# Normalisations on GpSimd, the values' bias through the output projection, and the gate in the output weights

## What is computed

```python
mod = (silu(c) @ wmod).reshape(4, 6, 1, 256)
sa, ca, ga, sb, cb, gb = mod[:, 0], ..., mod[:, 5]
ga = (2 * (ga >= 0) - 1) * maximum(abs(ga), 0.25)         # gb likewise
h = layernorm(x) * (1 + ca) + sa
qkv = h @ Wqkv.T + bqkv                                    # causal softmax attention per head
x = x + ga * (attention(qkv) @ Wout.T + bout)
h = layernorm(x) * (1 + cb) + sb
x = x + gb * ffn(h)                                        # shared + top-1 of 8 experts
```

## Time and profile before

| | |
|---|---|
| median of 3 runs | 481.53 us (480.63 to 483.06) |
| the profiled execution | 479.8 us |
| its span, first to last instruction | 478.1 us |
| first exponential of blocks 0, 1, 2, 3 | 69.55, 121.81, 183.48, 237.13 us |
| mean granted TensorE clock | 0.967 |
| busy: TensorE, VectorE, ScalarE, GpSimd | 402.4, 310.0, 226.8, 209.0 us |

### The profile page before, as it was taken

The page is one execution under the profiler, slowest core; times in us unless marked ns, Lnnn a source line. Parts: engine busy times, 40 slices in busy tenths (PEclk is TensorE's granted clock), DMA queues, the critical chain, the costliest instruction groups (busy, mean ns, idle before and its releaser), DMA issues.

```text
span 478.1 us, 8357 instructions
## 1 busy us (share of the span) xinstructions
PE 402.4 (84%) x2898; PEld 227.9 (48%) x2898; DVE 310.0 (65%) x629; ACT 226.8 (47%) x403; POOL 209.0 (44%) x251
## 2 busy tenths in 40 slices
PE   3767677889978789988879968999968999999991
PEld 3233233444544345444434434565645666666661
DVE  3823697876898968999977753789734444444441
ACT  2533424867666666755677636345122232323220
POOL 1457393374226763358331762110600555555332
PEclk9997789999999999998999989999989999999998
DMA  8568548765678557652433001994621344434210
GB/s 258 170 154 212 147 117 259 265 196 136 168 264 293 156 127 167 222 179 88 169 81 99 2 0 52 354 360 161 180 86 44 65 80 85 78 74 81 32 21 0
DMA packets 45921, 67.95 MB, mean 142 GB/s; under 512 B 5365, under 2 KB 33653, under 8 KB 45881
## 3 DMA queue, kind: packets, MB, share of 16 engines
q1 hardware_dynamic: 40200, 58.76, 40.6%
q0 software_dynamic: 5152, 8.14, 8.6%
q10 hardware_dynamic: 528, 0.52, 0.3%
HBM read 43.14 MB, written 25.18 MB: 143 GB/s over the span
## 4 chain that ended last, share of the span: by engine, by line
PE 51%; DVE 17%; DMA 8%; POOL 7%; issue 7%; ACT 6%; SPq 3%; ACTq 0%; DVEq 0%; POOLq 0%
PE bank L1411 35%; DVE mx L1066 5%; PE bank L1525 4%; PE bank L1509 3%; DVE rowg L1167 2%; PE bank L1739 2%; PE bank L1481 2%; DMA qk_d<-W 2%; POOL W L719 2%; DMA w_d<-rowg 2%; DMA mod_d<-h2T 1%; ACT rowg L896 1%; DMA stage<-in_gup 1%; POOL rowg L727 1%; POOL rowg L726 1%
## 5 line engine op out<-in xcount | busy, mean ns | idle before, releaser
L846 ACT ACTIVATE W<-bank 128x512 f32<-128x512 f32 (+1 forms) x176 | 94.8, 564 | 65.1 <-PE bank L1509 63.3
L1066 DVE TENSOR_REDUCE mx<-bank 128x1 f32<-128x384 f32 (+3 forms) x176 | 104.8, 632 | 20.2 <-PE bank L1483 19.9
L1411 PE MATMUL bank<-W 128*128 128x256 f16 (+2 forms) x756 | 106.5, 293 | 10.2 <-POOL W L694 3.4
L1411 PEld LDWEIGHTS bank<-W 128*128 128x128 f16 x756 | 73.3, 100 | 44.3 <-issue 14.2
L1481 PE MATMUL bank<-W 126*128 126x128 f16 (+3 forms) x256 | 67.0, 318 | 20.6 <-DVE mx L1066 17.2
L719 POOL TENSOR_SCALAR_AFFINE_SELECT W<-W 128x512 f32<-128x512 f32 x64 | 45.3, 713 | 79.7 <-ACT W L846 79.7
L1411 PE MATMUL bank<-W,h2T 128*128 x276 | 68.4, 385 | 4.9 <-DVE W L1182 4.0
L1509 PE MATMUL bank<-W 128*128 128x512 f16 (+3 forms) x256 | 63.1, 304 | 5.2 <-ACT W L846 3.5
L789 POOL DMA_INDIRECT out<-h2T,sidx x23 | 36.3, 1578 | 69.5 <-DVE h2T L1381 69.2
L1525 PE MATMUL bank<-W 128*32 128x128 f32 (+3 forms) x512 | 48.4, 451 | 8.7 <-POOL W L719 8.7
L1483 PE MATMUL bank<-maskb,identb 128*128 128x128 bf16 (+2 forms) x176 | 45.3, 257 | 0.0
(11 more groups left out here) (163 smaller groups left out, 522.7 us busy)
## 6 DMA issues: line engine op xcount, KB each, us to landing
w_d<-rowg SPq DMA_DIRECT2D x18, 512.0 KB, 3.9
W<-w_d SPq DMA_DIRECT2D x18, 512.0 KB, 8.0
stage<-in_gup SPq DMA_DIRECT2D x16, 512.0 KB
qk_d<-W SPq DMA_DIRECT2D x48, 128.0 KB
W<-qk_d SPq DMA_DIRECT2D x32, 192.0 KB, 4.4
stage<-in_down SPq DMA_DIRECT2D x8, 512.0 KB
x_sb<-in_x SPq DMA_DIRECT2D x4, 512.0 KB, 8.9
h_d<-gbb SPq DMA_DIRECT2D x4, 512.0 KB, 4.5
```

The costliest lines, as they stand in the source:

```text
L846: a.activation(PT[j][:, i:i + m, :], t_bank(N)[:, 0:m * w].rearrange("p (i n) -> p i n", i=m), ACT.Exp).then_inc(s_exp, 1)
L1066: v.tensor_reduce(mx_v[:, b % 2, hp0 // 4, par, i:i + m, t], SB[N % 3][:, 0:m * w].rearrange("p (i n) -> p i n", i=m), AX.X, ALU.max).then ...
L1411: i = t_.matmul(outp, l, r, start=(n == 0), stop=(n == len(prods) - 1), **kw)
```

## The change

- `norm1` runs on GpSimd, for all four batches, right behind its own `rstd`.
- `scale2` no longer has a part on VectorE; GpSimd's `modulate2` normalises the tile itself, so it has three instructions a tile and a link between each two. The last batch stays on VectorE.
- `v_out` runs on ScalarE, one instruction of 512 columns per part and without bias. The broadcast load of the values' bias is gone. Instead TensorE multiplies the bias by Wout (`value_bias`, two float32 products of 256 columns, ahead of the loop), and VectorE adds the result to `boutb`.
- A new side job `gate` at unit 26, batch b: GpSimd multiplies the output weights by the gate row (512 columns), ScalarE copies the high half, GpSimd makes the low half. The residual is then a single instruction. ScalarE no longer makes `wo16` itself but a float32 copy of the scaled weights, and VectorE's low half of them is gone.

```diff
-        (20, "bias", 0, 0), (37, "h2", -1, 0), (39, "h2", -1, 1),
+        (20, "bias", 0, 0), (26, "gate", 0, 0), (37, "h2", -1, 0), (39, "h2", -1, 1),
...
-            sp.dma_start(bvb, bqkv[2 * H:3 * H].partition_broadcast(P)).then_inc(s_bias, 16)
...
+            def norm1(b):
+
+                po.wait_ge(s_rstd, b + 1)
+                if b:
+                    po.wait_ge(s_xt, KC * b)
+                for t in range(TT):
+                    n = TT * b + t
+                    g.tensor_scalar(xn[:, t], x_sb[:, n], mv1[:, n, 0:1], rs1[:, n:n + 1],
+                                    ALU.subtract, ALU.mult).then_inc(s_xn, 1)
...
+            def gate_weights(b):
+
+                po.wait_ge(s_wh, 2)
+                po.wait_ge(s_bc[b % 2], 16 * (b // 2 + 1))
+                g.tensor_tensor(wog[:, :, :], wo32[:, :, :], bc[:, b % 2, 0:H].unsqueeze(1).to_broadcast([P, KC, H]),
+                                ALU.mult).then_inc(s_wg, 1)
+                po.wait_ge(s_wgh, b + 1)
+                g.tensor_tensor(wo16[:, 1], wog[:, :, :], wo16[:, 0], ALU.subtract).then_inc(s_wgl, 1)
...
-                po.wait_ge(s_hm, TT * b + t + 1)
+                n = TT * b + t
+                if t == 0:
+                    po.wait_ge(s_rstd2, b + 1)
+                    if b:
+                        po.wait_ge(s_ht, KC * b)
+                link(g.tensor_scalar(h2f[:, t], x_sb[:, n], mv2[:, n, 0:1], rs2[:, n:n + 1],
+                                     ALU.subtract, ALU.mult))
                 link(g.tensor_tensor(h2f[:, t], h2f[:, t], bc[:, b % 2, 2 * H:3 * H], ALU.mult))
                 g.tensor_tensor(h2f[:, t], h2f[:, t], bc[:, b % 2, H:2 * H], ALU.add).then_inc(s_h2, 1)
...
-                a.activation(wo16[:, 0], wo_s, ACT.Copy, scale=WS).then_inc(s_wh, 1)
+                a.activation(wo32[:, :, :], wo_s, ACT.Copy, scale=WS).then_inc(s_wh, 1)
...
+            def v_out(b, k):
+                ac.wait_ge(s_qkv, 6 * b + 5 + k)
...
+                dst = v1[b % 2][:, NH * 17 * 2 * k:NH * 17 * 2 * (k + 1)].rearrange("p (t h d) -> p t h d", t=2, d=17)
+                a.activation(dst[:, :, :, 0:HD], M1[:, :].rearrange("p (t h d) -> p t h d", t=2, d=HD), ACT.Copy,
+                             scale=1.0 / WS).then_inc(s_v, 2)
+
+            def gate_high(b):
+                ac.wait_ge(s_wg, b + 1)
+                if b:
+                    ac.wait_ge(s_o, TT * b)
+                a.activation(wo16[:, 0], wog[:, :, :], ACT.Copy).then_inc(s_wgh, 1)
...
                     for job, c, k in side_jobs(b, n):
-                        if job == "turn":
+                        if job == "v":
+                            v_out(c, k)
+                        elif job == "gate":
+                            gate_high(c)
+                        elif job == "turn":
                             h_parts(c, k)
...
             def low_others():
+                ve.wait_ge(s_bv, 1)
+                ve.wait_ge(s_bias, 32)
+                v.tensor_tensor(boutb, boutb, OTb[:, 0:H], ALU.add).then_inc(s_bo, 1)
                 ve.wait_ge(s_wh, 3)
-                v.scalar_tensor_tensor(wo16[:, 1], wo_s, WS, wo16[:, 0], ALU.mult, ALU.subtract)
...
-                    link(v.scalar_tensor_tensor(o1[:, t], side_bank("out", b, k)[:, H * (t % 2):H * (t % 2 + 1)],
-                                                1.0 / WS, bc[:, b % 2, 0:H], ALU.mult, ALU.mult))
-                    v.tensor_tensor(x_sb[:, n], x_sb[:, n], o1[:, t], ALU.add).then_inc(s_x2, 1)
+                    v.scalar_tensor_tensor(x_sb[:, n], side_bank("out", b, k)[:, H * (t % 2):H * (t % 2 + 1)],
+                                           1.0 / WS, x_sb[:, n], ALU.mult, ALU.add).then_inc(s_x2, 1)
...
+            def value_bias():
+                pe.wait_ge(s_wo, 32)
+                pe.wait_ge(s_bias, 32)
+                for k in range(KC):
+                    i = t_.matmul(OTb[:, 0:H], bqk[:, 4 + k:5 + k].to_broadcast([P, P]), wo_s[:, k], start=(k == 0),
+                                  stop=(k == KC - 1))
+                i.then_inc(s_bv, 1)
...
             def output(b, half):
                 pe.wait_ge(s_atl, KC * (b + 1))
+                pe.wait_ge(s_wgl, b + 1)
...
             modulation_rows()
+            value_bias()
```

More of the change, by code:

```diff
@@ L106, in side_jobs, with build @@
     return jobs
-def build(nc, x, wqkvT, bqkv, bqkc, woutT, bout, rwT, gup, down, sgw, suw, sdw, cT, wmod, out):
+def build(nc, x, wqkvT, bqkc, woutT, bout, rwT, gup, down, sgw, suw, sdw, cT, wmod, out):
     ctx = ExitStack()
@@ L130, in build @@
         rowg = sb("rowg", [P, RG, 2 * H])
-        o1 = rowg[:, 4:6, :].rearrange("p r (t n) -> p (r t) n", t=2)
-        h2f = o1
+        h2f = rowg[:, 4:6, :].rearrange("p r (t n) -> p (r t) n", t=2)
         h2s = rowg[:, 6:8, :].rearrange("p r (t n) -> p (r t) n", t=2)
@@ L223, in build @@
         q32 = h32
-        bvb = early(H)
+        at[0] += 2 * H
         qk16 = early(4 * 2 * S, F16).rearrange("p (a c n) -> p a c n", a=4, c=2)
@@ L236, in build @@
         bc = early(2 * 3 * H).rearrange("p (r n) -> p r n", r=2)
+        wo32 = early(KC * H).rearrange("p (k n) -> p k n", k=KC)
+        wog = early(KC * H).rearrange("p (k n) -> p k n", k=KC)
         assert at[0] <= (E + 1) * WX
@@ L300, in build @@
         s_v = sem("s_v")
+        s_bv = sem("s_bv")
+        s_wg = sem("s_wg")
+        s_wgh = sem("s_wgh")
+        s_wgl = sem("s_wgl")
+        s_bo = sem("s_bo")
         s_xb = sem("s_xb")
@@ L737, in _ @@
             rstd(ve1, mv1, rs1, 0, s_mv, s_rstd)
+            norm1(0)
             h_low(0, 0)
@@ L753, in _ @@
                             rstd(ve1, mv1, rs1, c, s_mv, s_rstd)
+                        elif job == "norm1":
+                            norm1(c)
                         elif job == "turn":
@@ L837, in qk_parts @@
                                  scale=1.0 / WS if isk else 0.25 / WS).then_inc(s, 1)
+            def v_out(b, k):
+                ac.wait_ge(s_qkv, 6 * b + 5 + k)
+                if k == 0 and b < 2:
+                    ac.wait_ge(s_const, 3 + b)
+                if k == 0 and b >= 2:
+                    ac.wait_ge(s_pv, 16 * (b - 1))
+                dst = v1[b % 2][:, NH * 17 * 2 * k:NH * 17 * 2 * (k + 1)].rearrange("p (t h d) -> p t h d", t=2, d=17)
[6 more added lines that the diff above has]
+                a.activation(wo16[:, 0], wog[:, :, :], ACT.Copy).then_inc(s_wgh, 1)
             def exps(N):
@@ L1012, in stats1 @@
                 i.then_inc(s_mv, 1)
-            def norm1(b):
-                ve.wait_ge(s_rstd, b + 1)
-                ve.wait_ge(s_mv, b + 1)
-                if b:
-                    ve.wait_ge(s_xt, KC * b)
-                for t in range(TT):
-                    n = TT * b + t
-                    v.tensor_scalar(xn[:, t], x_sb[:, n], mv1[:, n, 0:1], rs1[:, n:n + 1],
-                                    ALU.subtract, ALU.mult).then_inc(s_xn, 1)
-            def v_out(b, k):
-                ve.wait_ge(s_qkv, 6 * b + 5 + k)
-                if k == 0 and b < 2:
-                    ve.wait_ge(s_const, 3 + b)
-                if k == 0 and b >= 2:
-                    ve.wait_ge(s_pv, 16 * (b - 1))
-                for t in (2 * k, 2 * k + 1):
-                    dst = v1[b % 2][:, NH * 17 * t:NH * 17 * (t + 1)].rearrange("p (h d) -> p h d", d=17)
-                    src = M1[:, H * (t % 2):H * (t % 2 + 1)].rearrange("p (h d) -> p h d", d=HD)
-                    v.scalar_tensor_tensor(dst[:, :, 0:HD], src, 1.0 / WS,
-                                           bvb.rearrange("p (h d) -> p h d", d=HD),
-                                           ALU.mult, ALU.add).then_inc(s_v, 1)
             def modulation_columns():
                 ve.wait_ge(s_mc, 1)
-                ve.wait_ge(s_bias, 48)
+                ve.wait_ge(s_bias, 32)
                 v.tensor_copy(sac[:, :, :], T2[:, 0:8].rearrange("p (k b) -> p k b", k=KC))
@@ L1219, in _ @@
             stats1(0)
-            norm1(0)
             modulation_columns()
@@ L1517, in values @@
                     pe.wait_ge(s_v, TT * (b + 1))
-                if j == 0 and G:
-                    pe.wait_ge(s_ote, G)
+                if j == 0:
+                    pe.wait_ge(*((s_ote, G) if G else (s_bo, 1)))
                 pe.wait_ge(s_msk, 4 * G + j + 1)
@@ L1778, in _ @@
                     down_rows(r - 1, offs[r - 1])
-_INS = ["x", "wqkvT", "bqkv", "bqkc", "woutT", "bout", "rwT", "gup", "down", "sgw", "suw", "sdw", "cT", "wmod"]
+_INS = ["x", "wqkvT", "bqkc", "woutT", "bout", "rwT", "gup", "down", "sgw", "suw", "sdw", "cT", "wmod"]
 def kernel(L0_attn_x, L0_attn_Wqkv, L0_attn_bqkv, L0_attn_Wout, L0_attn_bout, L0_ffn_router_w,
```

29 lines of the change are left out of this document (9 added, 20 removed).

## The result

| | before | changed |
|---|---|---|
| median of 4 runs | 481.18 us | 504.40 us |
| lowest to highest | 480.63 to 483.06 | 501.20 to 506.35 |
| profiled execution, its span | 479.8, 478.1 | 503.09, 501.3 |

The ratio is 1.0469, with a 95% interval from 1.0402 to 1.0536. The change costs 23.2 us. I had forecast 487 us, 476.5 at best and 492.5 at worst: the direction was right, the size was not.

The account below looks back on a forecast made before the run. It took TensorE and VectorE as the two full engines; block costs 2.2 + (4.5 + 1.6 - 4.2) + (2.3 - 0.3) + 1.3 = 7.4 us on the profiled 479.8 gave 487 us, range 476.5 to 492.5.

Parts of the forecast that it names:

- What GpSimd gets: Normalisations moved to GpSimd: 0.48 us each, 0.72 for the range; 16 + 12 of them add 13.4 us there.
- norm1(0) ends near 9.8 us: At the start: GpSimd finishes before TensorE reaches its transposes at 11.11 us, so no cost; 0.3 us without that cover.
- hole of GpSimd that is 3.29 us long: After unit 10's mask, ahead of unit 14's: hides norm1(2) and norm1(3) at no cost; without it 1.9 us each.
- 2.0 to 2.1 us: Units 25 to 31: length of one modulate2 on GpSimd, three instructions and two links; 2.1 us taken.
- The stop of ScalarE: Unit 26: ScalarE waits for GpSimd's gate product, delaying exponentials; +2.2 us in block 0, +4.5 in block 1, +2.3 in block 2.
- The clock: Block 1, behind TensorE's 4.4 us hole: some 3 us of work at about half speed, +1.6 us.
- Block 3: Last attention block: mask at 280.9 us against 279.7, when TensorE took it after a 4.38 us wait; +1.3 us.
- C: Blocks 0 to 3: GpSimd and VectorE exclude each other, some six meetings of 1.0 us, half on the path; +3 us, 490; chance 0.13.
- VectorE's relief: TensorE holes ended by VectorE shrink: -4.2 us in block 1, gains of 1.2 in block 2 and 0.6 in block 3.
- The small edits: Value evictions on ScalarE, value_bias, one broadcast load less, bias into boutb: costed together at nothing.
- D: Blocks 1 and 3: GpSimd normalisations at 0.72 us, three ahead of each last mask; 488.5 us; chance 0.45 together with the forecast.
- A: Unit 26: ScalarE's wait is covered, so relief wins; 474.7 us against the profile, 476.4 against the median; chance 0.28.

Follow-up runs that it names:

- e1: The changed kernel with its 28 GpSimd normalisations as multiply, add instead of subtract, multiply: 491.76 us, +9.6 us against before.
- e6: The changed kernel with only the first batch's norm1 back on VectorE: 499.65 us, +17.2 us against before.
- e11: The changed kernel with norm1(0) and second normalisations back on VectorE, norm1(1) to (3) on GpSimd as multiply, add, gate product at unit 16: 478.64 us.
- e5: The changed kernel with only the second normalisation back on VectorE: 495.42 us, +12.9 us against before.
- e4: The changed kernel without the gate and with all normalisations back on VectorE, so only the values' part is left: 480.47 us, -1.7 us against before.
- e3: The changed kernel with all 28 GpSimd normalisations back on VectorE, gate and values' part kept: 489.84 us, +7.6 us against before.
- e7: The changed kernel with GpSimd's gate product moved from unit 26 to 16 and its low half to unit 28: 494.96 us, +12.5 us against before.
- e8: The changed kernel with GpSimd's normalisations as multiply, add and the gate's product at unit 16: 485.19 us, +2.9 us against before.
- e14: e11 with its GpSimd normalisations as add, multiply, so only the negated mean is prepared: 477.20 us, -3.3 us against before.

## Why the prediction was wrong, by its steps

**The step that failed** is the price in "What GpSimd gets": "The nearest row is L735, 0.48 us with one ... I take 0.48, as the only tensor_scalar of that size", with 0.72 as the other bound. It measured 1.33 and 1.22 us, and the prediction's own sign of being wrong, over 0.8 us, was met. With the cheap pair the change is at +9.6 us instead of +23.2 (e1). Three things hung on the price.
- "norm1(0) ends near 9.8 us ... so it costs nothing." It ended at 14.1, and norm1(0) on VectorE again gave 6.0 us (e6).
- norm1(2) and norm1(3) "lie in a hole of GpSimd that is 3.29 us long". Four dear ones take 4.85 us and delay the mask and the transposes; four cheap ones of 2.18 us do fit (e11).
- modulate2 "2.0 to 2.1 us". It is 2.8 and its links (1.22, with 0.83 and 0.76 for its two other instructions), and the second normalisation in this form cost 10.3 us (e5).

The two bounds were the fault behind the fault: both came from instructions of the right size with other operations. The rows with other operations (1.07 us at 256 elements; the earlier trace rows left them out) would have put the upper bound at 1.1 us or above. And with the right pair a normalisation takes 0.56 and not 0.48, for its second scalar.

**What held, and what did not.** e1, with 0.56 to 0.62 us a normalisation, is the kernel that I costed. By the first exponential of each block and the last of all, the blocks took:

| | first exponential | block 0 | block 1 | block 2 | block 3 |
|---|---|---|---|---|---|
| before | 69.6 | 52.2 | 61.7 | 53.6 | 58.6 |
| e1 | 69.1 | 54.2 | 63.3 | 56.3 | 62.6 |
| difference | -0.5 | +2.0 | +1.6 | +2.7 | +4.0 |
| forecast | 0 | +2.2 | +1.9 | +2.0 | +1.3 |
| e4 | 68.8 | 52.6 | 61.2 | 53.2 | 58.7 |
| e3 | 69.5 | 55.2 | 65.1 | 53.9 | 60.2 |
| the change | 72.1 | 57.8 | 67.0 | 57.0 | 62.7 |
| e11 | 70.0 | 52.5 | 59.4 | 52.5 | 59.2 |

- **The stop of ScalarE** was read well. I named 1.5 us in block 0 and over 3 in block 1; it is 1.63 and 4.44. The low clock that I put behind it is there at 0.50. Without the stop, 10.7 us come back (e7). It hardly depends on the price: in e1 it is 16.9 us.
- **The clock** was the other term that was mis-sized. I had +1.6 us for it, in block 1 alone. In the change TensorE's busy time grew by 11.9 us, 1.1 of them value_bias. In e1, at the right price, it grew by 6.1 (408.5 us), and the four blocks have 1.5, 1.7, 1.2 and 2.0 us of it. Block 1's is what I forecast; the others are not in the sum. For blocks 0 and 3, before and then e1 (columns as in the windows above):

```profile
69.60:121.80 52.20, 45.55 (x358) 21.87 (x356) 39.94 (x77) 36.26 (x64) 24.86 (x33) 1.00 0.70 205
237.10:295.70 58.60, 49.60 (x399) 25.48 (x400) 39.74 (x77) 36.12 (x67) 25.84 (x35) 0.97 0.18 52
...
69.10:123.30 54.20, 47.00 (x358) 22.54 (x356) 37.57 (x69) 37.79 (x68) 30.75 (x41) 0.97 0.67 205
242.90:305.50 62.60, 51.61 (x398) 25.96 (x399) 35.07 (x69) 36.68 (x68) 30.22 (x43) 0.92 0.17 52
```

  So about half of block 3's 4.0 us, and of block 2's 2.7, is TensorE at a lower clock, where I had none.
- **Block 3** was under-costed in the same way even at the right price: +4.0 in e1 for +1.3. I took TensorE's mask wait of the earlier trace rows as cover, and ScalarE waits 5.78 us there in e1. Which of its followers is the late one, no run tells. The sum had a slip there of 0.1 us, since 280.9 less 279.7 is 1.2, and the top of the range one of 0.8: C's 490 and 1.7 make 491.7, not 492.5. Neither changes anything.
- **VectorE's relief.** The holes behind L1095, the residual and the value evictions are gone from the list of waits. The one behind L1088 stays (1.9 us in two waits). In e11, with nothing else in the way, block 1 is 2.3 us shorter than before, where I had 4.2, and block 2 1.1, where I had 1.5. Block 3 is 0.6 longer. TensorE's order goes on to the next thing that is late, and of what the change moved that is GpSimd's masks: 13.2 us of waits in e11 for 8.7 in the old kernel.
- **The small edits** cost nothing, as forecast: e4 is 1.7 us faster than before. ScalarE's value evictions take 0.60 us each and value_bias 1.13 us of TensorE.
- **The rivals.** D was the right rival with the wrong price. A, the relief wins at 476.4, needed the wait at unit 26 covered. e8 covers it, with the cheap pair as well, and is at 485.19, 2.9 us above before, for the masks are late. e14 comes near A's time (477.2), but it leaves norm1(0) and the second normalisations on VectorE, so it does not bear A out. C costed six meetings of VectorE and GpSimd in the blocks, at 1.0 us each. The price was about right: in e1 one normalisation of block 1, beside VectorE's L1198, took 1.52 us where its like take 0.56. The count was not: in the change no normalisation in the blocks took over 1.51 us. The dear meeting is at the start, norm1(0)'s fourth instruction at 2.73 us for 1.21. The Trainium skill, SBUF — State Buffer, section "SBUF: two separate sides", has the two exclude each other for a whole instruction when VectorE's has two SBUF inputs, and this row agrees with it: the excess of 1.5 us is what was left of L1080.

A second page bears on the price. The Trainium skill, GPSIMD Engine Reference, section "4.1 Engine selection", has GpSimd's one-input operations at roughly line rate, where it weighs GpSimd against VectorE. For multiply with add (0.56 us against 0.41 for VectorE's normalisation, 1.4 times) that is not far from what is measured; for subtract with multiply (1.22 to 1.33) the measurement differs and decides.
